# The reciprocal of an attention denominator: VectorE's reciprocal instruction in place of logarithm, exponential and a refining step

## The reference

```
e  = exp(clip(W + K, -20, 10))            # W: decay by the distance to the last token
eu = exp(clip(U + K, -20, 10))
A  = shift(cumsum(e * V)) + eu * V
B  = shift(cumsum(e)) + eu
out = (sigmoid(R) * A / B) @ Wo.T + bo
```

## Time and profile before

| | |
|---|---|
| runs shown | 2075.43 us median of 3 (2075.39 to 2077.91) |
| the profiled execution | 2075.5 us, its span 2073.7 us |
| VectorE busy over the span | 1757.3 us (85%) |
| TensorE, GpSimd, ScalarE busy | 1553.3, 1171.4, 1042.3 us |
| a turn of the loop (turns 3 to 7) | 230.8 us |
| `v_wkv` in the run | 64 (8 tiles x 8 sequences) |

### The profile page before, as it was taken

The page is one execution under the profiler, slowest core; times in us unless marked ns, Lnnn a source line. Parts: engine busy times, 40 slices in busy tenths (PEclk is TensorE's granted clock), DMA queues, the critical chain, the costliest instruction groups (busy, mean ns, idle before and its releaser), DMA issues. The chain is left out here.

```text
span 2073.7 us, 21710 instructions
## 1 busy us (share of the span) xinstructions
PE 1553.3 (75%) x4800; PEld 732.6 (35%) x4800; DVE 1757.3 (85%) x2430; ACT 1042.3 (50%) x1572; POOL 1171.4 (56%) x939
## 2 busy tenths in 40 slices
PE   5163486579896898679896898679896879788858
PEld 2020133134442353334442353244443344345434
DVE  4198888999998999989998999979998999875462
ACT  2345345554664557555663557545664444343321
POOL 0448636854685557754685648754686655442240
PEclk8575587679998999899997999889998999899979
DMA  4442433442335143332335143423335223311200
GB/s 138 149 145 99 153 98 107 137 132 92 119 130 173 52 133 126 121 126 94 118 117 181 51 132 123 152 92 101 112 117 170 91 70 97 89 51 38 64 31 26
DMA packets 167632, 225.19 MB, mean 109 GB/s; under 512 B 13457, under 2 KB 104082, under 8 KB 167506
## 3 DMA queue, kind: packets, MB, share of 16 engines
q1 hardware_dynamic: 167506, 223.99, 33.0%
HBM read 179.90 MB, written 39.85 MB: 106 GB/s over the span
## 5 line engine op out<-in xcount | busy, mean ns | idle before, releaser
L646 POOL TENSOR_TENSOR bu<-rep,bc 128x512 f32<-128x512 f32 x512 | 643.2, 1283 | 292.7 <-PE ps_y L1132 247.8
L943 DVE TENSOR_TENSOR_SCAN ps_d<-ps_d,bu 128x512 f32<-128x512 f32 x512 | 623.9, 1220 | 16.1 <-ACT ps_d L775 8.7
L775 ACT ACTIVATE ps_d<-rep,scale_a 128x512 f32<-128x512 f32 x512 | 348.5, 686 | 384.2 <-DVE bu L950 346.6
L1083 PE MATMUL ps_r<-xT,wgu 128*128 128x512 f32 x768 | 372.6, 625 | 54.1 <-ACT kv L804 30.7
L950 DVE TENSOR_TENSOR bu<-ps_d,bc 128x512 f32<-128x512 f32 x512 | 344.5, 674 | 0.0
L1132 PE MATMUL ps_y<-bu,sel 128*32 128x512 f32 x1024 | 173.2, 755 | 155.2 <-DVE bu L950 154.9
L1083 PE MATMUL ps_r<-mix,wkv 128*128 128x512 f32 x512 | 258.5, 643 | 34.2 <-DVE xr L897 16.0
L658 POOL TENSOR_TENSOR kv<-sums,kv 128x1024 f32<-128x1024 f32 x64 | 150.6, 2353 | 231.7 <-DVE sums L1039 223.6
L1083 PEld LDWEIGHTS ps_r<-xT,wgu 128*128 128x128 f32 x768 | 146.7, 199 | 269.4 <-issue 238.0
L1083 PE MATMUL ps_r<-mix,wr 128*128 128x512 f32 x256 | 159.5, 757 | 73.7 <-ACT yr L813 32.0
L681 ACT ACT_TABLE_LOAD x122 | 156.5, 1283 | 58.9 <-PE ps_r L1083 38.9
(11 more groups left out here) (102 smaller groups left out, 2088.7 us busy)
## 6 DMA issues: line engine op xcount, KB each, us to landing
rep<-dd_scratch SPq DMA_DIRECT2D x128, 512.0 KB, 4.5
wgu<-gu_scratch SPq DMA_DIRECT2D x96, 256.0 KB, 2.8
dd_scratch<-xs SPq DMA_DIRECT2D x32, 512.0 KB, 3.5
bc<-bc_scratch SPq DMA_DIRECT2D x64, 256.0 KB, 5.0
win<-w_in_dram SPq DMA_DIRECT2D x64, 128.0 KB, 2.2
xc_scratch<-xc SPq DMA_DIRECT2D x32, 256.0 KB, 3.0
sz_scratch<-xin SPq DMA_DIRECT2D x32, 256.0 KB, 2.1
xg<-xc_scratch SPq DMA_DIRECT2D x32, 256.0 KB, 3.5
```

Source lines behind the costliest of these rows:

```text
L646: pool.tensor_tensor(bu[:, i % BU, :], rep[:, g % REP, 1, :], bc[:, 0, q, :], ALU.mult)\
L775: act.activation(ps_d[D_BANK[i]][:, :], rep[:, g % REP, 0, :], ACT.Exp, scale=scale_a[:, a, NQ * j + q:NQ * j + q + 1]).then_inc(decay_rea ...
L943: dve.tensor_tensor_scan(d[:, :], d[:, :], bu[:, i % BU, :], 0.0, ALU.mult, ALU.add)\
L1083: last = pe.matmul(dst, lhs, rhs, start=n == 0, stop=n == len(pairs) - 1)
```

## The change

The units `a_rec` are gone from ScalarE, with their table loads. `v_wkv` waits for `dn_ready` itself, takes the reciprocal of the denominator in place by one VectorE instruction, and multiplies it by the numerator with a second one. Both operands of that product now lie in SBUF. Orders, banks and waits of the other units stay; `a_rec` stays in the bank lists, so that the follower in a bank still waits for `wkv_ready`.

```
-                    elif unit == "a_rec":
-                        act.wait_ge(dn_ready.sem, at(dn_ready, r, i + 1))
-                        rec = take(act, unit, i, t)
-                        need("natural_log_exp_and_others")
-                        act.activation(rec[:, :], kv[:, row(i, "eu"), :], ACT.Ln).then_inc(ln_ready.sem, 1)
-                        act.wait_ge(ln_ready.sem, at(ln_ready, r, i + 1))
-                        act.activation(rec[:, :], rec[:, :], ACT.Exp, scale=-1.0).then_inc(rec_ready.sem, 1)
...
-                        den, num, rec = kv[:, row(i, "eu"), :], kv[:, row(i, "euv"), :], ps_r[BANK["a_rec", i]]
-                        dve.wait_ge(rec_ready.sem, at(rec_ready, r, i + 1))
-                        dve.tensor_tensor(den, den, rec[:, :], ALU.mult).then_inc(newton.sem, 1)
-                        dve.wait_ge(newton.sem, at(newton, r, 2 * i + 1))
-                        dve.scalar_tensor_tensor(rec[:, :], den, 2.0, rec[:, :], ALU.subtract, ALU.mult)\
-                            .then_inc(newton.sem, 1)
-                        dve.wait_ge(newton.sem, at(newton, r, 2 * i + 2))
+                        den, num = kv[:, row(i, "eu"), :], kv[:, row(i, "euv"), :]
+                        dve.wait_ge(dn_ready.sem, at(dn_ready, r, i + 1))
+                        dve.reciprocal(den, den).then_inc(inverted.sem, 1)
+                        dve.wait_ge(inverted.sem, at(inverted, r, i + 1))
                         dve.wait_ge(num_gated.sem, at(num_gated, r, i + 1))
-                        dve.scalar_tensor_tensor(yr[:, i, :], rec[:, :], -1.0, num, ALU.mult, ALU.mult)\
-                            .then_inc(wkv_ready.sem, 1)
+                        dve.tensor_tensor(yr[:, i, :], den, num, ALU.mult).then_inc(wkv_ready.sem, 1)
```

More of the change, by code:

```diff
@@ L374, in hybrid_block @@
         num_gated = signal("num_gated", CT)
-        ln_ready = signal("ln_ready", CT)
-        rec_ready = signal("rec_ready", CT)
-        newton = signal("newton", 2 * CT)
+        inverted = signal("inverted", CT)
         wkv_ready = signal("wkv_ready", CT)
```

## The result

The changed kernel took 2205.15 us in the median of 4 runs (2202.28 to 2205.45), the kernel before 2076.67 (4 runs): ratio 1.0615, interval 1.0597 to 1.0634, or +128 us. Forecast were 2190 us and a range of 2145 to 2265, so +114.6 us where +128 were measured. The profiled execution has a span of 2203.5 us, against 2073.7.

What follows compares the result with a forecast made beforehand. VectorE's order was taken as the clock in turns 3 to 8, a chain across engines in turns 9 and 10. +93.5 and +21.1 make +114.6 us on 2075.5: forecast 2190 us, range 2145 to 2265.

Steps and rivals of the forecast that it cites:

- The sign and the cause: Whole kernel: slower, chance 0.84, because the reciprocal lengthens VectorE's order, the clock in turns 3 to 8.
- The reciprocal's duration: VectorE's new reciprocal of 128 x 512: taken as 3.40 us, between ends of 0.67 and 4.50 us.
- four bits a round: VectorE's divider: a 24-bit quotient found four bits at a time holds the pipe six steps a column, 3.40 us.
- The lower end of the frame: Reciprocal on VectorE at one step a column, like a product: 0.67 us, nothing with 512 columns being cheaper.
- Eight rounds: Rival: VectorE's reciprocal holds the pipe eight steps a column, 4.50 us, giving 2257 us; chance 0.24.
- Turns 3 to 8: 48 of the 64 `v_wkv`, +96.5 us on VectorE, less 3.0 us of waits for ScalarE: +93.5 us.
- The pair: Reciprocal, gap and product in each `v_wkv` on VectorE: 4.05 us against 2.04, so +2.01 us each.
- The waits for ScalarE that go: VectorE's waits for ScalarE's half of the reciprocal in turns 3 to 8: 0.6 us a turn, -3.0 us.
- Turns 9 and 10: 13 of 16 `v_wkv` count, 26.1 us, less 5.0 us of waits for ScalarE: +21.1 us.
- one round: Rival: VectorE's reciprocal costs what a product does, 0.67 us, so the change pays, 2021 us; chance 0.12.
- Each us taken out shortens it: Turns 3 to 8: VectorE is the clock, so time removed from its order shortens the turn, as added time lengthens it.
- the break-even: VectorE's reciprocal in `v_wkv`: the change's sign turns at a duration of 1.5 us, n = 2.5 steps a column.

Runs made afterwards that it cites:

- the two kernels on it: Changed kernel with ScalarE's logarithm, exponential and table loads kept, result unused: 2205.28 us; kernel before with them left out, three VectorE instructions kept: 2072.19 us.
- The halves: Changed kernel with each tile's reciprocal done in two instructions of 128 x 256: 2209.68 us, ratio 1.0655 to the kernel before.
- the plain instruction: Changed kernel with a multiplication by 1 in place instead of the reciprocal, so the output is not the quotient: 2078.56 us, ratio 1.0021 to the kernel before.
- PSUM: Kernel with a multiplication by 1 instead of the reciprocal, now writing to the logarithm's PSUM bank, which the product reads: 2050.14 us, ratio 0.9881 to the kernel before.
- the one with PSUM: Changed kernel with the reciprocal written to the logarithm's PSUM bank, so the product reads PSUM and SBUF: 2196.26 us, ratio 1.0579 to the kernel before.
- the one with ScalarE kept: Changed kernel with ScalarE's logarithm, exponential, table loads and VectorE's waits for them kept, result unused: 2205.28 us, ratio 1.0627 to the kernel before.
- the two fastest ones: Kernel before without its refining step, table loads ahead of ScalarE's waits: 2046.93 us; changed kernel with a multiplication by 1 into PSUM instead of the reciprocal: 2050.14 us.
- no refining: Kernel before without its refining step: ScalarE's logarithm and exponential, then one VectorE product from PSUM and SBUF: 2065.33 us, ratio 0.9942.

## Why the prediction was right, and where it was not

**The sign and the cause** were right. VectorE's order is the clock upwards, one instruction makes the whole difference, and neither what ScalarE is relieved of (the two kernels on it) nor GpSimd's or TensorE's slack hides any of it. One sign did not come: VectorE is busy for 94% of a turn (235.0 of 249.1 us), not for more than 95%, and waits stand in the place of those that went.

**The reciprocal's duration**, the number on which everything hung, was 3.33 us against the 3.40 taken. The choice between 0.67 and 4.50 rested on an argument from the scan's row and on four bits a round, and no run shows how the divider works; that it came out within 2% is luck in good part. The halves show only that the cost goes by the column, at 5.9 times that of a product's column. The lower end of the frame was misread as well: "nothing on VectorE with 512 columns is cheaper" than 0.67 us is contradicted by the kernel before itself, where L923, a TENSOR_SCALAR of 128 x 512, takes 542 ns, and by the plain instruction's 395 in place. Eight rounds of a product's column would be 4.50 us, so the repeat count of 8 in the Trainium skill ("VectorE: DVE Perf Modes", "Walkthrough: the 8-slice pipeline in each mode") can't be read as eight such rounds; the measurement decides.

**Turns 3 to 8: +93.5 forecast, +106.2 measured.** Laid side by side, instruction by instruction, the two traces give: the tiles +100.3 us, the running sums +3.5, all other instructions -1.1, the waits of VectorE +3.5. Three terms were mis-sized. The pair: 3.97 us alone as against 4.05, but 4.13 with the exclusion, which I had set at 0: 2.09 x 48 = 100, not 96.5. It had been seen in the earlier trace rows and put aside because the sums, with the same two operands, showed little of it; but four of eight products meet an instruction of GpSimd, and with the new timing one sum in each turn does too (L1024 of the seventh tile, 1.71 us for 1.22), which is most of the 3.5. The waits for ScalarE that go: 2 us, not 3. And the other waits, taken as unchanged: +5.5 on balance, with +6.8 for TensorE behind the fourth tile as the largest, and others shorter, the 4 us of turn 7 among them.

**Turns 9 and 10: +21.1 forecast, +24.9 measured.** 13 of 16 tiles were taken as counting; all sixteen did, 32.2 us instead of 26.1. The waits for ScalarE took off 6.0 instead of 5.0, and everything else 1.3.

**The rivals.** The one on the other side, one round, would have come out wrong in its own terms. "Each us taken out shortens it" is the step of the prediction that failed: I read VectorE's 95% as a bound in both directions. (The rival's 208 of 218 us a turn does not follow from its own sum either, which gives 230.8 - 8 x 0.72 - 0.6 = 224.) Taken downwards, a plain instruction gave 2079 us where the sum had 2021, first through the exclusion (28 us, shown by PSUM), then because other chains, over TensorE and over ScalarE's table loads, are close behind VectorE's order: no edit brought one of turns 4 to 7 below 228.4 us. So the break-even that I worked out, a reciprocal of 1.5 us, is wrong as well: with operands in SBUF even a plain instruction of 0.4 us does not win. Whether a shorter reciprocal would exclude GpSimd as the plain instruction did, is not known; the real one did not.

**Open.** The changed kernel, the one with PSUM, the one with ScalarE kept and the one with halves all have turns of 248.7 to 249.4 us in turns 5 to 7, though VectorE's own work in them differs by up to 1.4 us. Which chain holds that length is not settled. Nor is what holds 228.5 to 229 us in the two fastest ones: VectorE waits there a few us a turn, for TensorE, ScalarE and GpSimd in turn.

## What to carry to other kernels

VectorE's f32 reciprocal costs about as much a column as six columns of a product, so on an engine that is the clock, three plain instructions and ScalarE's two beside them are the cheaper way, and a reciprocal belongs on few columns. Work added to an engine at 94 to 95% lengthened the turn in full; how much a saving pays has to be read from the next chain, and here it was from an eighth (no refining) to two thirds (the plain instruction into PSUM). Two things cost little and are easy to miss: one operand of a VectorE instruction moved from SBUF to PSUM keeps it out of GpSimd's way, and a table load belongs ahead of ScalarE's wait, not behind it.

## What the runs showed of the hardware

- A reciprocal of 128 x 512 f32 took 3333 ns, of 128 x 256 1713 ns, and into PSUM 3341 ns; GpSimd's instructions ran beside it at their usual 1.26 and 2.35 us, though both its source and its result were in SBUF.
- A multiplication by a constant of the same tile in place took 395 ns at best and 885 in the mean (into PSUM 662 to 696, each time), since it and GpSimd exclude each other, and the product with two SBUF operands behind it 1373 in place of 691. Exclusion lengthens the instructions of both engines and shows in no wait of the profile, only in durations.
- With the same instructions on every engine, turns of one kernel differed by up to 4 us where TensorE's granted clock did: 234.9 us at 0.89 against 230.5 to 231.6 at 0.91 to 0.92 in the kernel before, 235.1 at 0.88 against 232.1 to 232.6 at 0.90 without refining. In the changed kernel, with VectorE the longest by more, they stayed within 0.3 us at 0.89 to 0.91.
